# A two-layer attention kernel: a reordered front with image 0 first and layer 2's weight products behind the first t products

## The reference

```
xn  = group_norm(x, 32 groups of 8 channels, over all positions) * gamma + beta
q   = xn @ wq + bq ;  k = xn @ wk + bk ;  v = xn @ wv + bv
out = softmax(q @ k^T / 16) @ v
x   = out @ wp + bp + x
```

## Time and profile before

| | |
|---|---|
| median of three runs | 253.14 us (253.07 to 253.24) |
| profiled execution, span | 250.6 us, 4585 instructions |
| PE (tensor engine) busy | 245.2 us, 98% |
| DVE (vector engine) busy | 187.2 us, 75% |
| ACT (ScalarE) busy | 149.4 us, 60% |
| POOL (GpSimd) busy | 125.1 us, 50% |
| chain that ended last, by engine | PE 89%, DVE 6%, DMA 2% |

### The profile page before, as it was taken

One profiled execution on the slowest core, in us unless ns is written; L12 is line 12 of the kernel. 1 busy time (PEld: TensorE's weight loads), 2 busy tenths in 40 slices (PEclk: granted clock), 3 DMA queues, 4 the chain that ended last, 5 costly groups with the idle time before them and its releaser, 6 DMA issues.

```text
span 250.6 us, 4585 instructions
## 1 busy us (share of the span) xinstructions
PE 245.2 (98%) x1570; PEld 223.5 (89%) x1570; DVE 187.2 (75%) x490; ACT 149.4 (60%) x291; POOL 125.1 (50%) x151
## 2 busy tenths in 40 slices
PE   7999998999999999999999999999999999999995
PEld 6888888889998899889998899889998899889995
DVE  0688898888994798587975998587875798449804
ACT  3665543699994309831998508940998509740920
POOL 3010621485779306901797916901797918800870
PEclk9999999999999999999999999999999999999999
DMA  6999000000025002320142001320110000100112
GB/s 195 352 153 221 6 0 3 0 1 3 0 86 86 1 0 55 84 32 3 43 87 43 0 0 46 84 41 3 43 43 0 3 16 29 42 0 10 36 42 86
DMA packets 34767, 12.37 MB, mean 49 GB/s; under 512 B 26284, under 2 KB 34488, under 8 KB 34744
## 3 DMA queue, kind: packets, MB, share of 16 engines
q1 hardware_dynamic: 34720, 12.07, 20.0%
q10 hardware_dynamic: 24, 0.01, 0.0%
HBM read 7.88 MB, written 4.19 MB: 48 GB/s over the span
## 4 chain that ended last, share of the span: by engine, by line
PE 89%; DVE 6%; DMA 2%; issue 1%; ACT 1%; SPq 0%; DVEq 0%
PE ring L1134 12%; PE ring L1136 12%; PE ring L1135 12%; PE ring L1109 10%; PE ring L1110 10%; PE ring L1108 10%; PE ring L1081 3%; PE ring L1083 3%; PE ring L1082 3%; PE ring L1094 3%; PE ring L1096 3%; PE ring L1095 2%; DVE R L732 2%; DMA xnat<-in_x 2%; PE ring L948 1%; DVE xraw L593 1%
## 5 line engine op out<-in xcount | busy, mean ns | idle before, releaser
L363 POOL TENSOR_TENSOR P_lo<-S,P_hi 128x512 fp32r<-128x512 f32 x64 | 81.9, 1310 | 52.2 <-ACT S L503 52.1
L1134 PE MATMUL ring<-V,P_hi 128*128 128x258 f32 x256 | 72.7, 284 | 0.0
L1136 PE MATMUL ring<-V,P_lo 128*128 128x258 f32 x256 | 72.4, 283 | 0.0
L1135 PE MATMUL ring<-V,P_hi 128*128 128x256 f32 x256 | 72.3, 282 | 0.0
L502 ACT ACTIVATE P_hi<-S 128x512 fp32r<-128x512 f32 x64 | 40.4, 631 | 29.7 <-DVE S L791 29.7
L495 ACT COPY S<-ring 128x512 f32<-128x512 f32 x64 | 36.6, 590 | 31.4 <-PE ring L1110 30.3
L1108 PE MATMUL ring<-t_hi,xn_lo 128*128 128x512 f32 x128 | 49.9, 390 | 0.0
L1109 PE MATMUL ring<-t_lo,xn_hi 128*128 128x512 f32 x128 | 49.8, 389 | 0.0
L1110 PE MATMUL ring<-t_hi,xn_hi 128*128 128x512 f32 x128 | 49.8, 389 | 0.0
L1134 PEld LDWEIGHTS ring<-V,P_hi 128*128 128x128 f32 x256 | 48.5, 189 | 0.4
L1135 PEld LDWEIGHTS ring<-V,P_hi 128*128 128x128 f32 x256 | 48.4, 189 | 0.4
(11 more groups left out here) (117 smaller groups left out, 356.3 us busy)
## 6 DMA issues: line engine op xcount, KB each, us to landing
xnat<-in_x SPq DMA_DIRECT2D x8, 256.0 KB, 4.6
between<-xnat SPq DMA_DIRECT2D x16, 128.0 KB, 1.8
out<-xnat SPq DMA_DIRECT2D x16, 128.0 KB, 1.7
moved<-in_x SPq DMA_DIRECT2D x8, 128.0 KB, 4.7
moved<-between SPq DMA_DIRECT2D x16, 64.0 KB, 2.4
moved<-between SPq DMA_DIRECT2D x32, 32.0 KB, 2.0
w_wq<-in_L_conv_wq SPq DMA_DIRECT2D x2, 256.0 KB, 4.3
w_wk<-in_L_conv_wk SPq DMA_DIRECT2D x2, 256.0 KB, 4.5
```

The costliest lines, as they stand in the source:

```text
L363: nc.gpsimd.tensor_tensor(P_lo[:, exp_of(c, kb), :], S[:, tile_of(c, kb), :], P_hi[:, exp_of(c, kb), :].bitcast(F32), ALU.subtract).then_i ...
L1134: nc.tensor.matmul(bank[:, 0:C + 2], P_hi[:, tile, mine], v[:, kb, 0:C + 2], start=(kb == 0), stop=False)
L1135: nc.tensor.matmul(bank[:, 0:C], P_hi[:, tile, mine], v[:, kb, C + 2:VX], start=False, stop=False)
L1136: last = nc.tensor.matmul(bank[:, 0:C + 2], P_lo[:, tile, mine], v[:, kb, 0:C + 2], start=False, stop=(kb == NB - 1))
```

## The change

In the front the change does these things.

- SP loads image 0 first, then wq, wk, the broadcast rows, wv and wp of layer 1, then all of layer 2. The broadcast rows (wide) take bp too, three rows instead of two.
- The tensor engine transposes image 0 before any weight. Each piece keeps a bank of its own, and the vector engine reads bn_stats from that bank; ScalarE copies raw x to SBUF after it.
- The affine map has fewer dependent steps: var + eps times r0 squared in one operation, r0 times gamma beside it, and shift = beta - mean * gain as one operation per channel block.
- ScalarE makes the hi part of image 0 straight from raw x with gain and shift, while the vector engine writes normalised x to S for the lo part. The first t product of a half takes the matmuls with the hi part of x first.
- bv wp is formed on GpSimd as rows (weighted_rows: two scalings of wp's rows by bv, their sum, its rounded part, the rest) and summed over partitions by two matmuls with a matrix of ones; bp is added from the broadcast rows. The small bias matmuls and transposes go.
- Layer 1's Wx and all of layer 2's transposes and products come after the first t products.
- The vector engine takes image 1's statistics before the running maxima of the first half instead of among them.

The diff, cut to its core:

```diff
@@ SP, loads @@
+            load_image(0)
             load_weights(0, ("wq", "wk"))
-            load_image(0)
+            load_wide(0)
             load_weights(0, ("wv", "wp"))
-            load_weights(1, ("wq", "wk"))
-            load_wide(0)
-            load_weights(1, ("wv", "wp"))
+            load_weights(1, ("wq", "wk", "wv", "wp"))
             load_wide(1)
@@ GpSimd @@
+            def weighted_rows(l):
+
+                r = l * NV + VECTORS.index("bv")
+                pool.wait_ge(ld_w[l, "wp"], 16)
+                for k in range(KC):
+                    nc.gpsimd.tensor_scalar(weighted[:, l, k, :], w_raw[l, "wp"][:, k, :], vec_cols[:, k, r:r + 1],
+                                            None, ALU.mult).then_inc(po_bv, 1)
+                pool.wait_ge(po_bv, 5 * l + 2)
+                nc.gpsimd.tensor_tensor(weighted[:, l, 0, :], weighted[:, l, 0, :], weighted[:, l, 1, :], ALU.add
+                                        ).then_inc(po_bv, 1)
+                pool.wait_ge(po_bv, 5 * l + 3)
+                nc.gpsimd.tensor_copy(weighted_hi[:, l, :], weighted[:, l, 0, :]).then_inc(po_bv, 1)
+                pool.wait_ge(po_bv, 5 * l + 4)
+                nc.gpsimd.tensor_tensor(weighted_lo[:, l, :], weighted[:, l, 0, :], weighted_hi[:, l, :].bitcast(F32),
+                                        ALU.subtract).then_inc(po_bv, 1)
...
+            weighted_rows(0)
             power(0)
+            weighted_rows(1)
             pool.wait_ge(dv_ob, 1)
@@ ScalarE @@
             def raw_rows(r, bank):
-                act.wait_ge(pe_xT, r + 1)
+                act.wait_ge(dv_bn, r + 1)
...
+                    act.wait_ge(dv_stat, SHIFT)
+                    nc.scalar.activation(xn_hi[:, k, cols], xraw[:, k, cols], ACT.Identity, bias=shift[:, k:k + 1],
+                                         scale=gain[:, k:k + 1]).then_inc(ac_xh, 1)
@@ vector engine @@
             def statistics_of(v, r):
                 if v == 0:
-                    dve.wait_ge(ac_xT, r + 1)
+                    dve.wait_ge(pe_xT, r + 1)
+                    for k in range(KC):
+                        last = nc.vector.bn_stats(bn[:, k, r, :], ring[r][:, 2 * k * P:2 * (k + 1) * P])
+                    last.then_inc(dv_bn, 1)
+                    return
...
             group_deviation(0)
-            A_low(0, 0)
             variance(0)
-            A_low(0, 1)
             affine_map(0)
-            normalise(0, range(0, 2))
-            Wx_low(0, 0)
+            for k in range(KC):
+                A_low(0, k)
+            for q in range(2):
+                normalise_first(q)
             xn_low(0, 0)
+            attention_vector(0, 0)
             xn_low(0, 1)
...
             for k in range(KC):
+                Wx_low(0, k)
+            for k in range(KC):
+                t_low(0, 1, k)
+            statistics_of(1, 0)
+            for k in range(KC):
                 A_low(1, k)
+            statistics_of(1, 1)
+            for k in range(KC):
+                Wx_low(1, k)
+            output_biases()
+            statistics_of(1, 2)
+            statistics_of(1, 3)
+            channel_statistics(1)
             attention_vector(0, 2)
...
@@ tensor engine @@
+                pe.wait_ge(po_bv, 5 * LAYERS)
+                nc.tensor.matmul(ring[RING - 1][:], ones[:], weighted_hi[:, :, :].rearrange("p l c -> p (l c)"),
+                                 start=True, stop=False)
+                nc.tensor.matmul(ring[RING - 1][:], ones[:], weighted_lo[:, :, :].rearrange("p l c -> p (l c)"),
+                                 start=False, stop=True).then_inc(pe_oa, 1)
...
+                if u == 0 and k == 0:
+
+                    for kc in range(KC):
+                        pe.wait_ge(ac_xh, h * KC + kc + 1)
+                        nc.tensor.matmul(bank[:], A_lo[:, l, kc, mine], xn_hi[:, kc, cols], start=(kc == 0), stop=False)
+                        nc.tensor.matmul(bank[:], A_hi[:, l, kc, mine], xn_hi[:, kc, cols], start=False, stop=False)
+                    for kc in range(KC):
+                        wait_for_x_low(pe, u, h * KC + kc + 1)
+                        last = nc.tensor.matmul(bank[:], A_hi[:, l, kc, mine], xn_lo[:, kc, cols],
+                                                start=False, stop=(kc == KC - 1))
```

More of the change, by code:

```diff
@@ L124, in two_attention_layers @@
         eps = sb("eps", [P, LAYERS])
[L125 removed]
+        ones = sb("ones", [P, P], F32R)
         out_bias = sb("out_bias", [P, LAYERS, C])
@@ L575, in _ @@
             nc.vector.memset(minus_half[:], -0.5)
+            nc.vector.memset(ones[:].bitcast(F32), 1.0)
             for v in V:
@@ L621, in attention_vector @@
                                                accum_out=att[:, l, n:n + 1]).then_inc(dv_att, 1)
[L623 to L627, removed]
             def output_biases():
                 dve.wait_ge(pe_oa, 1)
-                nc.vector.tensor_copy(out_bias[:, :, :], ring[RING - 1][:, :].rearrange("p (l c) -> p l c", l=LAYERS)
-                                      ).then_inc(dv_ob, 1)
+                for l in range(LAYERS):
+                    dve.wait_ge(ld_wide[l], 16)
+                    last = nc.vector.tensor_tensor(out_bias[:, l, :], ring[RING - 1][:, l * C:(l + 1) * C],
+                                                   wide[:, l, WIDE.index("bp"), :], ALU.add)
+                last.then_inc(dv_ob, 1)
             def channel_statistics(v):
@@ L642, in group_deviation @@
                 dve.wait_ge(pe_gm, v + 1)
[L643 removed]
                 dve.wait_ge(dv_stat, at + AGGR)
                 nc.vector.tensor_tensor(dev[:], mv[:, :, 0], mean_bank(v), ALU.subtract).then_inc(dv_stat, 1)
+                nc.vector.tensor_scalar(less_mean[:], mean_bank(v), -1.0, None, ALU.mult)
                 dve.wait_ge(dv_stat, at + DEV)
[L647 to L649 removed]
+                for k in range(KC):
+                    last = nc.vector.scalar_tensor_tensor(var_c[:, k:k + 1], dev[:, k:k + 1], dev[:, k:k + 1],
+                                                          mv[:, k, 1:2], ALU.mult, ALU.add)
+                last.then_inc(dv_stat, 1)
             def variance(v):
@@ L666, in affine_map @@
-                dve.wait_ge(dv_stat, at + RSTD)
-                nc.vector.tensor_tensor(gain[:], rstd[:], gamma, ALU.mult).then_inc(dv_stat, 1)
-                dve.wait_ge(dv_stat, at + GAIN)
[L669 to L678, removed]
-                                            ALU.mult, ALU.add).then_inc(dv_xn, 1)
+                for k in range(KC):
+                    last = nc.vector.scalar_tensor_tensor(r0sq[:, k:k + 1], r0[:, k:k + 1], r0[:, k:k + 1],
+                                                          var_e[:, k:k + 1], ALU.mult, ALU.mult)
@@ new lines, in affine_map @@
+                last.then_inc(dv_stat, 1)
+                nc.vector.tensor_tensor(r0_gamma[:], r0[:], gamma, ALU.mult)
+                dve.wait_ge(dv_stat, at + R0SQ)
+                nc.vector.tensor_scalar(factor[:], r0sq[:], -0.5, 1.5, ALU.mult, ALU.add).then_inc(dv_stat, 1)
+                dve.wait_ge(dv_stat, at + FACTOR)
+                nc.vector.tensor_tensor(gain[:], factor[:], r0_gamma[:], ALU.mult).then_inc(dv_stat, 1)
+                dve.wait_ge(dv_stat, at + GAIN)
+                for k in range(KC):
+                    last = nc.vector.scalar_tensor_tensor(shift[:, k:k + 1], less_mean[:, k:k + 1], gain[:, k:k + 1],
+                                                          beta[:, k:k + 1], ALU.mult, ALU.add)
@@ L681, in xn_low, with normalise_first @@
+                last.then_inc(dv_stat, 1)
+            def normalise_first(q):
+                h, k = divmod(q, KC)
+                dve.wait_ge(ac_xT, 2 * (h + 1))
+                dve.wait_ge(dv_stat, SHIFT)
+                nc.vector.tensor_scalar(S[:, q, :], xraw[:, k, h * BANK:(h + 1) * BANK], gain[:, k:k + 1],
+                                        shift[:, k:k + 1], ALU.mult, ALU.add).then_inc(dv_xn, 1)
             def xn_low(v, q):
@@ L954, in Wx_product @@
                 pe.wait_ge(ld_w[l, "wp"], 16)
-                bank = ring[2 + mc][:, 0:C] if l == 0 else X[:, mc * C:(mc + 1) * C]
+                bank = X[:, mc * C:(mc + 1) * C]
                 for kd in range(KC):
@@ L1164, in _ @@
                 t_product(0, 0, k)
-            Wx_product(1, 1)
+            for mc in range(KC):
+                Wx_product(0, mc)
+            transpose_weight(1, 0)
+            transpose_weight(1, 1)
             for k in range(KC):
                 t_product(0, 1, k)
+            transpose_weight(1, 2)
+            for mc in range(KC):
+                A_product(1, mc)
+            for mc in range(KC):
+                Wx_product(1, mc)
             output_biases_to_all()
```

172 lines of the change are left out of this document (66 added, 106 removed).

## The result

The changed kernel takes 262.92 us (median of four runs, 262.30 to 263.64) against 253.12 us (253.07 to 253.24; 253.14 was the median of the first three of these four runs) before: a ratio of 1.039, 95% interval 1.0374 to 1.0405. The medians are of all runs of a kernel, and the ratios leave out runs in a slow state, over 1.5% above the kernel's fastest, among them one of e2 and one of e6 near 1375 us. The forecast was 258.3 us, with a range up to 260.8. Slower was right; the loss is about twice as large as forecast, 9.8 us for 5.2. The profiled execution spans 260.7 us, 10.1 us more: the first score comes 9.8 us later, the stretch behind it is 0.9 us shorter, and the rest of the execution 1.2 us longer.

What follows compares the result with a forecast made beforehand. The tensor engine, busy with both layers' weights, was taken to bound the front. First score 5.55 us later, less 0.66 of waiting, plus 0.3 for the clock: +5.2 on 253.14, giving 258.3 us, range 255.2 to 260.8.

Steps and rivals of the forecast that it cites:

- the moved work: Tensor engine, between t and the scores: 5.96 us of weight work formerly done ahead of t, with nothing covering it.
- wp: Loads: layer 1's wp lands at 11.2 us, between 10.9 and 11.4, behind the larger broadcast rows.
- GpSimd, the first step that failed: Five new instructions on wp take 3.0 us (2.5 to 3.9) ahead of the power, which starts at 14.2 us.
- The affine chain: Vector engine: four dependent steps, two split into columns, take 0.9 us; shift ready at 15.9 us.
- xn_low: Vector engine, image 0's lo part: 0.60 us a step, the second done at 19.2 us.
- The clock: Tensor engine at half clock when t starts after the gap; cost taken as 0.3 us.
- Rival B: Clock stays low through t and Wx, costing 2 to 3.4 us more: 260 to 261.4 us; chance 0.15.
- The gap: Tensor engine idle 3.65 us ahead of t, from near 13.0 to 16.65 us.
- rival A: GpSimd's new work does not hold r0; the variance decides, r0 at 12.2, time 255.3 us; chance 0.1.
- no wait for neg_shift: Among the first half's values, the tensor engine's 0.66 us wait for the vector engine goes.
- The output biases: Third score's bank release: ready a few tenths before it is asked for; if late, by up to 0.5 us.
- Nothing different after 50 us but the offset: Rest of the execution after 50 us: unchanged apart from being shifted in time.

Runs made afterwards that it cites:

- e2: Changed kernel with only layer 2's weighted rows on GpSimd moved behind image 0's second xn_low; 261.89 us, 1.034 of the kernel before.
- e6: On e3, the tensor engine runs the variance and layer 1's A products ahead of wv's transposes; 255.53 us, 1.008 of the kernel before.
- e5: Changed kernel with layer 1's Wx, layer 2's wq and wk transposes and A products back ahead of t; 258.63 us, 1.021 of the kernel before.
- e4: Changed kernel with 16 unused small matmuls between layer 1's A products and the first t; 261.29 us, 1.032 of the kernel before.
- e8: On e7, wv's transposes ahead of the variance again, layer 2's wq and wk loaded before the broadcast rows and transposed before t; 251.61 us, ratio 0.995.
- e7: On e6, broadcast rows loaded behind wp and layer 1's Wx put ahead of t; 253.09 us, 1.001 of the kernel before.
- e9: Kernel before with only the output biases made the new way, GpSimd's rows behind the second xn_low; 254.50 us, ratio 1.006.
- e1: Changed kernel with GpSimd's power for image 0 ahead of both layers' weighted rows; 261.10 us, 1.031 of the kernel before.
- e3: Changed kernel with GpSimd's power first and both layers' weighted rows behind image 0's second xn_low; 258.37 us, 1.023 of the kernel before.

## Why the prediction was wrong, step by step

- Direction, and the moved work: right. From the end of t's second bank to the first score the forecast had 9.8 us (30.6 - 20.8, that is 19.4 + 1.41); measured 34.88 - 25.13 = 9.75. e5 shows that it stands on the path.
- wp: its first user starts at 11.91, for 11.2. That misses by 0.7 (the dearer bound was 11.4). In e4, with the same load order, it starts at 13.07.
- **GpSimd, the first step that failed.** The five instructions take 3.88 us, not 3.0; that is the dearer bound (3.9). A scaling of 128x256 by a column was put at 0.45 near the affine select; it takes 0.92, more than the two-input operations (0.72). Only the cast is at 0.40. The Trainium skill (GPSIMD Engine Reference, section 4.1) has one-input work roughly at line rate; the scaling does not agree. So the power starts at 15.79 instead of 14.2.
- **The affine chain, the second.** Put at 0.9 us, it took 1.74, for two reasons: the split columns cost 0.35 a pair, where a single step takes 0.16 and the forecast added 0.07 for the second start, so that even undisturbed (e2, e6) the chain takes 1.13, hardly less than the old one's 1.15 (13.72 to 14.87); and GpSimd beside it adds 0.6. The forecast put layer 2's rows, which start with the chain, at nothing, without a reason. The Trainium skill (Trainium Architecture — The Big Picture, What this means for kernel authors) says that the vector engine and GpSimd contend for a shared port pair; the rows agree that they slow each other (also GpSimd's: two scalings 1.84 alone, 2.69 beside xn_low in e8); that it is at this port pair, no run shows.
- xn_low: counted at 0.60 a step; the first takes 1.14, for the same reason. The second ends at 22.17 instead of 19.2.
- **The clock, the third.** Half clock was expected when t starts, and happened; taken at 0.3 us, "as the engine is busy nearly all the time from 16.65". But the busy engine did not have the clock back at once: t starts at 19.28, and the clock stayed at 0.50 until 24.8. t's second bank alone lost 0.9, the matmul ahead of it 0.4; e4 puts the cost at 1.2. Rival B's mechanism was right through t, though not through Wx, and the price lies below its 2 to 3.4.
- The gap: 3.84 us for 3.65, which is luck. Its start was forecast near 13.0 and came at 15.45, as wv landed later than worked out in rival A and the A products ran at the lower level (3.07 us instead of 1.84); its end came 2.6 us late.
- The sum ahead of the score: 0.7 (wp) + 0.9 (GpSimd) + 0.8 (chain) + 0.6 (xn_low) + 1.3 (clock in t) is the 4.3 by which the first score missed 30.6. GpSimd is the largest part: the 0.9, some 0.6 of the chain's 0.8, and the 0.6 of xn_low.
- After the score: the stretch from the first score to scores(1) is 0.91 us shorter (18.05 for 18.96), forecast 0.66; no wait for neg_shift, as said. The output biases were not late.
- "Nothing different after 50 us but the offset": wrong. From scores(1) to the end the changed kernel takes 1.2 us more (207.8 for 206.6). 0.67 is the tensor engine's wait for image statistics at 180 us, behind a store. The chain of waits after:

```profile
162.66 3.74 DMA between<-xnat
...
171.14 1.82 DMA between<-xnat
```

  Two equal stores, 3.74 and 1.82 us. SP's longest wait for such a store is 1.7 us before and 3.4 after. The same wait shows in e2, e7, e8 and e9, not in e1, e3, e4, e5 and e6, so it belongs to no single edit; in these nine kernels the stretch takes 206.6 to 208.1 us. Why a store takes longer in some executions stays open, as do the other 0.5 us.

## What to carry to other kernels

Ask first what the bounding engine does while it waits for a result: an earlier result is worth nothing if the work that filled the wait is moved behind it (e5, e8). A new instruction on an idle engine is not free when it stands ahead of a small step that others wait for, or beside one on a neighbour that slows down with it. And an idle gap can be paid twice, in time and in the clock of what follows (1.2 us in e4); whether it is, depended here on more than its length (e1, e6).

## What was not expected of the hardware

- GpSimd: scaling 128x256 by a column takes 0.92 us, adding two tensors of that size 0.72, a rounding copy 0.40.
- The vector engine's 128x2 steps go from 0.16 to 0.66 us beside GpSimd's 128x256 additions (e9), and from 0.16 to 0.41 beside its scalings.
- The granted clock was 0.50 when work resumed at 19.28 after the 3.84 us gap, and stayed there until 24.8 us. Three other runs had gaps of nearly one length ahead of t: 1.33 us in e1, where the clock was 0.50 already; 1.37 in e3, where it fell to 0.50 at 17 us, within t; and 1.48 in e6, where it stayed at 1.00. In the changed kernel it was also low from 7.8 to 14.5 us, behind waits of 1.3 us for x; there the A products took 3.07 instead of 1.98 us (e6), hidden behind r0.
- In one load order, GpSimd's first scaling, which waits for wp, starts between 11.91 (after) and 13.07 us (e4).
